# Attention scores from two fp32r parts on alternating 64-row halves of TensorE, with the maxima's product in front of the scores in each step

## The chip, the core and the metric

The kernel runs on one NeuronCore of a Trainium2 chip. The core has TensorE (matrix products, PE), VectorE (DVE), ScalarE (ACT), GpSimd (POOL) and SyncE (SP, which here only starts transfers), an on-chip memory of 128 partitions (SBUF) and eight accumulator banks (PSUM) that TensorE writes. The metric is the device time of one execution in microseconds (us), lower is better; the time before is the median of three runs.

## What is computed

The input is 16 images of 128 channels and 32 x 32 positions, so 1024 tokens per image. A group normalisation with a channel gate comes first, then attention with 8 heads of 16 dimensions, then a mixture of 8 experts of which each token takes two. The part that matters here, shortened from the reference:

```python
qkvt = x @ W_qkv                        # x: (16, 1024, 128), after a layer norm
q, k, v, t = jnp.split(qkvt, 4, axis=-1)
q, k, v, t = map(to_heads, (q, k, v, t))            # 8 heads of 16
dots = jnp.einsum('bhid,bhjd->bhij', q, k) * scale  # 16 ** -0.5
attn1 = jax.nn.softmax(dots, axis=-1)
out1 = jnp.einsum('bhij,bhjd->bhid', attn1, v)
# out2: t smeared with fixed weights exp(-|i-j|/e); out = [out1, out2] @ W_out + b_out
```

## The kernel before, in words

**Stages.** From about 76 to 1966 us the kernel works on attention, one image after the other. The experts follow, as 71 blocks of 512 token rows, and a last pass adds the results. The expert products already use the type fp32r, with 128 x 128 weights and 512 columns (L978 to L980).

**Scores before.** The fp32 values of q and k are split into three bf16 parts each. Six products of parts make up one score, and they are stacked along the contraction: 6 x 16 = 96 rows (`SHIFT_ROW`), plus 3 rows for the row maximum in three parts against ones (`STACK` = 99). So one product on 96 or 99 rows gives an fp32-like score. The split is made by `split` on GpSimd (four passes over 128 x 1024 for q, four for k; VectorE does it for image 0). SP writes the parts to DRAM (`rows_to_dram`) and reads them back as stacks (`load_stacks`), since they change partitions on the way.

**Each score is computed twice.** `full_scores` (L825) computes one unit, one head and 128 queries against all 1024 keys, as two products of 512 columns into one of two bank pairs; `maximum` (VectorE, L1359) reduces the unit to its row maxima. 64 units make an image. After 32 units `turn_maxima` turns the maxima (L832), `shift` (VectorE) splits them, and `load_shift` (SP) writes them into the query stack as extra rows. `scores` (L845) then computes the transposed scores less the maximum, two products of 512 columns per step into two banks, `weights` (ScalarE, L1114) takes the exponential of each, and `values` (L857) multiplies every two steps the four probability tiles with the values: four fp32 products on 32-column tiles of the array, next to each other (eight records in the trace, as fp32 products with 128 x 512 operands show up as two parts).

**Order.** All engines follow an order written out by hand. An image has 64 steps. In step s of image `it` TensorE issues `scores(it, s + 1)` (two products), the unit of maxima that lies 40 steps ahead (two products), in odd steps `values`, and then side work by tables: transposes of 4 x 128 columns in steps 0, 2 (`turn_x`), 4 (`turn_o`), 6, 8 (`back_o`), 12, 14 (`back_n`), 42, 44 (`turn_t2`), 48, 50, 52 (`turn_o`); the dispatch product in 62; 512-column fp32 products in 16, 18 (q), 20, 22 (k), 32, 36 (`project_out`), 54 to 60 (`values_and_z`, two of them as four 128-column products); small ones in 25 and 57 (`turn_maxima`) and 53 (logits). A side result goes through the one side bank and is copied out by ScalarE or VectorE two to four steps later. A pair of steps, in this text, reaches from the end of one `values` group to the end of the next; the side work of an even step stands in its middle.

**Waits around the change.** A score product waits until the exponential has read its bank (`exp_done`). A unit of maxima waits until the unit two before it is reduced (`max_done`). The first score product of each half image waits for the shift rows (`shift_in`). `projected` (ScalarE, L1079) copies q and k out of the side bank for `split`.

Of the kernel before, what the change touches and what calls it, by code (L numbers as in the profile page):

```python
# [7 lines left out]
F32 = mybir.dt.float32  # L8
BF16 = mybir.dt.bfloat16
# [6 lines left out]
P = 128  # L16
# [21 lines left out]
PAIRS = 6  # L38
SHIFT_ROW = PAIRS * DH
STACK = SHIFT_ROW + 3  # L40
# [61 lines left out]
DCT_Y = (0, 1, 0, -1, 3, 0, 2, 0)  # L102

# [81 lines left out]
def build(nc, a, out):  # L185
# [3 lines left out]
    with ExitStack() as ctx:  # L189
# [46 lines left out]
        max_parts = sb("max_parts", [GROUP_ROWS, 3, P], BF16)  # L236
        max_rest = sb("max_rest", [GROUP_ROWS, P])
# [15 lines left out]
        q_parts = sb("q_parts", [P, 3, TOK], BF16)  # L253
        k_parts = sb("k_parts", [P, 3, TOK], BF16)
# [5 lines left out]
        def stack(n):  # L260
            return big[0:STACK, n * BIG_Q:(n + 1) * BIG_Q].bitcast(BF16).rearrange("p (h t) -> p h t", h=HEADS)

# [74 lines left out]

        q_rows = dram("q_rows", (PAIRS, P, TOK), BF16)
        k_rows = dram("k_rows", (PAIRS, P, TOK), BF16)
# [10 lines left out]
        memset_done = sem("memset_done")  # L350
        root_done = sem("root_done")
# [20 lines left out]
        qk_split = sem("qk_split")  # L372
        rows_out = sem("rows_out")
# [62 lines left out]
        LATE_INC = 16 * len(late_consts)  # L436
        CONST_INC = 16 * len(consts)
        ROWS_INC = PAIRS * 16
        STACK_INC = 2 * 16
        SHIFT_INC = 3 * 16  # L440
# [15 lines left out]
        def _(sp):  # L456
# [10 lines left out]
            def rows_to_dram(k):  # L467
                sp.wait_ge(qk_split, 2 * k + 1)
                if k:
                    for g in range(GROUPS):  # L470
                        sp.wait_ge(stack_in[(k - 1) % 2][g], ((k - 1) // 2 + 1) * STACK_INC)
                sp.dma_start(q_rows[0:3].rearrange("s p t -> p s t"),
                             q_parts[:, 0:1, :].broadcast_to([P, 3, TOK])).then_inc(rows_out, 16)
                sp.dma_start(q_rows[3:5].rearrange("s p t -> p s t"),
                             q_parts[:, 1:2, :].broadcast_to([P, 2, TOK])).then_inc(rows_out, 16)
                sp.dma_start(q_rows[5], q_parts[:, 2, :]).then_inc(rows_out, 16)
                sp.wait_ge(qk_split, 2 * k + 2)
                sp.dma_start(k_rows[0:3].rearrange("s p t -> p s t"), k_parts[:, 0:3, :]).then_inc(rows_out, 16)
                sp.dma_start(k_rows[3:5].rearrange("s p t -> p s t"), k_parts[:, 0:2, :]).then_inc(rows_out, 16)
                sp.dma_start(k_rows[5], k_parts[:, 0, :]).then_inc(rows_out, 16)  # L480

            def load_stacks(k, g):
                sp.wait_ge(rows_out, (k + 1) * ROWS_INC)
                if k >= 2:
                    sp.wait_ge(score_ready, 2 * (k - 2) * STEPS + (g + 1) * STEPS)
                heads = slice(g * GROUP, (g + 1) * GROUP)
                for stk, rows in ((q_stack, q_rows), (k_stack, k_rows)):
                    by_row = rows.rearrange("s (d h) t -> (s d) h t", h=HEADS)
                    sp.dma_start(stk[k % 2][0:SHIFT_ROW, heads, :],
                                 by_row[:, heads, :]).then_inc(stack_in[k % 2][g], 16)  # L490

            def load_shift(k, g):
                sp.wait_ge(max_split, 2 * k + g + 1)
                for j in range(3):
                    sp.dma_start(q_stack[k % 2][SHIFT_ROW + j:SHIFT_ROW + j + 1, g * GROUP:(g + 1) * GROUP, :]
                                 .rearrange("p h (t q) -> p (h t) q", q=P),
                                 max_parts[:, j, :]).then_inc(shift_in, 16)
# [86 lines left out]
        def _(pool):  # L584
# [7 lines left out]
            def clear(n):  # L592
                link(pool.memset(v_aug[n], 0.0))
                link(pool.memset(v_aug[n][:, :, :, DH:DH + 1], 1.0))
                link(pool.memset(k_stack[n][SHIFT_ROW:STACK, :, :], 1.0))
# [7 lines left out]

            link(pool.memset(minus_half[:, :], -0.5))
# [1055 lines left out]
```

## Time and profile before

| | |
|---|---|
| median of 3 runs | 2513.67 us (2505.27 to 2515.43) |
| profiled execution | 2517.94 us, span 2516.0 us |
| TensorE busy | 2175.5 us (86%) |
| VectorE busy | 1883.6 us (75%) |
| ScalarE busy | 1453.4 us (58%) |
| GpSimd busy | 1116.9 us (44%) |
| mean granted TensorE clock | 0.944 |

The profile is taken on one execution. Busy time of TensorE counts a product from its start to a modelled end, and successive products overlap in it, so the distance between starts tells more than the duration. What a group of instructions waited for is shown as idle time in front of it with the instruction that ended it.

### The profile page before, as it was taken

How to read it: one execution, taken by the hardware profiler on the slowest of the kernel's cores; microseconds unless marked ns; L12 is line 12 of the kernel's file. 1: busy time of each engine (PE TensorE's matmuls, PEld its weight loads, DVE VectorE, ACT ScalarE, POOL GpSimd, SP SyncE). 2: the span in 40 equal slices, each digit the busy share in tenths (PEclk: the TensorE clock that was granted, in tenths of full speed). 3: DMA queues.
4: the chain of work that ended last, by engine and by line, in shares of the span. 5: the costliest groups of instructions: out<-in, count | busy, mean ns of one | idle time of the engine just before them, and what ended most of it. 6: DMA issues, size and time to landing. Idle time of an engine off the chain costs nothing.

```text
span 2516.0 us, 33117 instructions
## 1 busy us (share of the span) xinstructions
PE 2175.5 (86%) x11552; PEld 897.6 (36%) x11552; DVE 1883.6 (75%) x2555; ACT 1453.4 (58%) x2833; POOL 1116.9 (44%) x1240
## 2 busy tenths in 40 slices
PE   2589999999999999999999999999999447778843
PEld 1223333323333333323233333333232136666633
DVE  7877888888888888888888888888882256666732
ACT  1157767767776767767776767666667213444420
POOL 4303316163544526162535435263142446777764
PEclk9889999999999999999999999999998668998975
DMA  5412222231313132231313132322012058666659
GB/s 182 133 43 77 66 79 91 80 110 30 107 35 102 44 102 74 79 106 31 110 33 104 36 101 68 93 74 64 17 52 76 26 170 286 208 195 201 213 172 341
DMA packets 109926, 264.83 MB, mean 105 GB/s; under 512 B 23048, under 2 KB 40912, under 8 KB 103184
## 3 DMA queue, kind: packets, MB, share of 16 engines
q1 hardware_dynamic: 87600, 217.77, 27.6%
q0 software_dynamic: 17280, 35.95, 4.1%
q10 hardware_dynamic: 4880, 8.99, 0.9%
q8 instruction: 92, 1.51, 0.3%
q14 instruction: 74, 0.61, 0.1%
HBM read 154.63 MB, written 111.56 MB: 106 GB/s over the span
## 4 chain that ended last, share of the span: by engine, by line
PE 57%; POOL 12%; ACT 10%; DMA 8%; DVE 5%; issue 5%; SPq 1%; ACTq 0%; POOLq 0%; DVEq 0%
PE ps L857 17%; PE ps L845 15%; PE ps L825 12%; ACT region L1114 8%; POOL y_dram L732 5%; PE ps L802 2%; DMA big<-w_dram 2%; DMA y_dram<-region 2%; DVE row_max L1359 2%; DMA region<-y_dram 2%; POOL norm_v L625 1%; POOL region L629 1%; POOL region L628 1%; ACT region L1121 1%; PE ps L889 1%
## 5 line engine op out<-in xcount | busy, mean ns | idle before, releaser
L1359 DVE TENSOR_REDUCE row_max<-ps 128x1 f32<-128x1024 f32 x1024 | 1239.7, 1220 | 270.8 <-PE ps L825 239.4
L1114 ACT ACTIVATE region<-ps 128x512 f32<-128x512 f32 x2048 | 1112.7, 596 | 528.9 <-PE ps L845 509.6
L845 PE MATMUL ps<-big 99*128 99x512 bf16 x2048 | 666.1, 387 | 44.4 <-DMA big<-max_parts 12.8
L825 PE MATMUL ps<-big 96*128 96x512 bf16 x2048 | 617.6, 383 | 29.6 <-DMA big<-k_rows 18.7
L857 PE MATMUL ps<-region 128*32 128x512 f32 x4096 | 551.1, 610 | 0.7 <-ACT region L1114 0.7
L845 PEld LDWEIGHTS ps<-big 99*128 99x128 bf16 x2048 | 159.8, 98 | 696.1 <-ACT region L1114 649.9
L732 POOL DMA_INDIRECT y_dram<-region x284 | 272.8, 960 | 126.2 <-issue 81.6
L617 POOL TENSOR_TENSOR norm_v<-norm 128x8 f32<-128x8 f32 x32 | 6.7, 210 | 650.2 <-DVE norm L1350 650.1
L676 POOL DMA_INDIRECT xs_dram<-region,slot x256 | 254.9, 996 | 81.2 <-issue 71.8
L825 PEld LDWEIGHTS ps<-big 96*128 96x128 bf16 x2048 | 199.4, 99 | 245.3 <-DVE row_max L1359 30.2
L978 PE MATMUL ps<-big 128*128 128x512 f32 x284 | 128.3, 452 | 73.1 <-DMA big<-w_dram 72.5
L1186 ACT ACTIVATE region<-ps,big 128x512 f32<-128x512 f32 x71 | 48.9, 689 | 209.2 <-PE ps L980 209.2
L857 PEld LDWEIGHTS ps<-region 128*32 128x32 f32 x4096 | 80.8, 108 | 215.6 <-issue 214.8
L1588 DVE TENSOR_SCALAR big<-ps,big 128x512 fp32r<-128x512 f32 x142 | 105.7, 745 | 34.2 <-PE ps L980 33.9
L1578 DVE TENSOR_TENSOR big<-ps,big 128x512 fp32r<-128x512 f32 x71 | 49.1, 692 | 97.1 <-ACT big L1180 78.0
L979 PE MATMUL ps<-big 128*128 128x512 f32 x284 | 120.9, 426 | 0.0
L980 PE MATMUL ps<-big 128*128 128x512 f32 x284 | 120.6, 425 | 0.0
L1591 DVE SCALAR_TENSOR_TENSOR big<-ps,big 128x512 fp32r<-128x512 f32 x142 | 106.6, 751 | 5.0
L651 POOL TENSOR_TENSOR chosen<-pick 128x64 bf16<-128x64 f32 x16 | 5.1, 319 | 209.9 <-DVEq L1451 209.9
L978 PEld LDWEIGHTS ps<-big 128*128 128x128 f32 x284 | 58.3, 205 | 96.7 <-DMA big<-w_dram 84.6
L1028 PE MATMUL ps<-ident,region 128*128 128x128 f32 x128 | 31.5, 428 | 63.0 <-POOL region L739 63.0
L1194 ACT ACTIVATE region<-ps,region 128x128 f32<-128x128 f32 x284 | 80.7, 373 | 4.1 <-DMA y_dram<-region 3.6
(195 smaller groups left out, 2189.4 us busy)
## 6 DMA issues: line engine op xcount, KB each, us to landing
big<-w_dram SPq DMA_DIRECT2D x71, 514.0 KB, 4.6
big<-q_rows SPq DMA_DIRECT2D x32, 768.0 KB, 5.7
big<-k_rows SPq DMA_DIRECT2D x32, 768.0 KB, 8.0
region<-xs_dram SPq DMA_DIRECT2D x71, 264.0 KB, 2.8
region<-y_dram SPq DMA_DIRECT2D x16, 1024.0 KB, 10.5
region<-in_x SPq DMA_DIRECT2D x28, 512.0 KB, 9.3
q_rows<-q_parts SPq DMA_DIRECT2D x16, 768.0 KB, 3.8
k_rows<-k_parts SPq DMA_DIRECT2D x16, 768.0 KB, 3.5
```

Of the source, the lines that this page charges most:

```text
L676: pool.indirect_dma_start(xs_dram[:, :], bass.IndirectOffsetOnAxis(ap=slot[:, n * TILES + t:n * TILES + t + 1], axis=0), n2_row[:, t, :], ...
L732: pool.indirect_dma_start(y_dram[:, :], bass.IndirectOffsetOnAxis(ap=xs[b % XS_BUFS][:, j, INDEX_COL:INDEX_COL + 1].bitcast(I32), axis=0), ...
L825: mm = pe.matmul(ps[:, M_BANK + 2 * (n % 2) + c, :], q_stack[k % 2][0:SHIFT_ROW, h, t * P:(t + 1) * P], k_stack[k % 2][0:SHIFT_ROW, h, c * ...
L845: pe.matmul(ps[:, E_BANK + i, :], k_stack[k % 2][:, h, t * P:(t + 1) * P], q_stack[k % 2][:, h, c * BANK:(c + 1) * BANK], start=True, stop ...
L857: mm = pe.matmul(ps[32 * r:32 * r + 32, O_BANK, :], v_aug[k % 2][:, t, g * GROUP + r, :], probs[:, u % 2, r, :], start=(t == 0), stop=(t = ...
L978: pe.matmul(dst, w[:, high_at:high_at + P], high, start=start, stop=False)
L979: pe.matmul(dst, w[:, high_at:high_at + P], low, start=False, stop=False)
L980: return pe.matmul(dst, w[:, low_at:low_at + P], high, start=False, stop=stop)
L1114: act.activation(probs[:, u % 2, 2 * p + i, :], ps[:, E_BANK + i, :], ACT.Exp, scale=DH ** -0.5).then_inc(exp_done, 1)
L1359: dve.tensor_reduce(row_max[:, n:n + 1], ps[:, at:at + 2, :], AX.XY, ALU.max).then_inc(max_done, 1)
L1588: dve.tensor_scalar(h_high[b % 2][f], src, w[:, NEG_B1 + f:NEG_B1 + f + 1], None, ALU.max).then_inc(h_high_done, 1)
L1591: dve.scalar_tensor_tensor(h_low[b % 2][f], src, w[:, NEG_B1 + f:NEG_B1 + f + 1], h_high[b % 2][f].bitcast(F32), ALU.max, ALU.subtract).th ...
```

## The change

The parts become fp32r: two parts of q and k (`PARTS`), three products of parts (`PAIRS`), so 48 rows, and 2 rows for the maximum (`STACK` = 50). The stacks are laid out in two halves (`LANES`): heads 0 and 1 of each group of four lie in partitions 0 to 49, heads 2 and 3 in 64 to 113. A product therefore addresses 64 rows by 128 columns of the array. `max_unit` reorders the units of maxima within half an image so that they alternate between the halves. In the loop of TensorE the first unit of maxima is issued by halves in front of the two score products: M, S, M, S.

ScalarE now rounds the first part straight from the side bank (`parts[:, 0]`) and then copies the full value, and takes over the wait for the last image's row transfers. GpSimd and, for image 0, VectorE only subtract. `shift` has two operations instead of four. The rows of ones come from a small tile by four transfers from ScalarE's queue, instead of GpSimd's memsets. The stacks are loaded in four transfers per call instead of two, the shift rows in four instead of three.

```diff
@@
-PAIRS = 6
+PARTS, PAIRS = 2, 3
+LANES = 2
+LANE = P // LANES
+LANE_HEADS = GROUP // LANES
 SHIFT_ROW = PAIRS * DH
-STACK = SHIFT_ROW + 3
+STACK = SHIFT_ROW + PARTS
@@
+def max_unit(n):
+    g, i = divmod(n, GROUP_ROWS)
+    lane = 1 - i % LANES
+    of_lane, t = divmod(i // LANES, TILES)
+    return g * GROUP + lane * LANE_HEADS + of_lane, t
@@ stacks
+        def lane_of(h):
+            return h % GROUP // LANE_HEADS
+        def lane_rows(stk, h, rows):
+            at = lane_of(h) * LANE
+            return stk[at:at + rows, h // GROUP * LANE_HEADS + h % LANE_HEADS, :]
@@ split, on GpSimd
-                if k:
-                    pool.wait_ge(rows_out, k * ROWS_INC)
-                link(pool.tensor_copy(parts[:, 0, :], full))
-                link(pool.tensor_tensor(full, full, parts[:, 0, :], ALU.subtract))
-                link(pool.tensor_copy(parts[:, 1, :], full))
-                pool.tensor_tensor(parts[:, 2, :], full, parts[:, 1, :], ALU.subtract).then_inc(qk_split, 1)
+                pool.tensor_tensor(parts[:, 1, :], full, parts[:, 0, :].bitcast(F32), ALU.subtract).then_inc(qk_split, 1)
@@ full_scores(unit, c): one half of a unit
+                h, t = max_unit(n)
...
+                mm = pe.matmul(ps[:, M_BANK + 2 * (n % 2) + c, :],
+                               lane_rows(q_stack[k % 2], h, SHIFT_ROW)[:, t * P:(t + 1) * P],
+                               lane_rows(k_stack[k % 2], h, SHIFT_ROW)[:, c * BANK:(c + 1) * BANK], start=True, stop=True)
@@ scores(k, s, i): one of the two products
+                h = g * GROUP + LANE_HEADS * p + i
...
+                pe.matmul(ps[:, E_BANK + i, :], lane_rows(k_stack[k % 2], h, STACK)[:, t * P:(t + 1) * P],
+                          lane_rows(q_stack[k % 2], h, STACK)[:, c * BANK:(c + 1) * BANK], start=True,
+                          stop=True).then_inc(score_ready, 1)
@@ the loop of TensorE
-                    if here and s + 1 < STEPS:
-                        scores(it, s + 1)
-                    if nxt and s + 1 == STEPS:
-                        scores(it + 1, 0)
-                    for unit in max_units(it, s):
-                        full_scores(unit // STEPS, unit % STEPS)
+                    units = list(max_units(it, s))
+                    for c in range(HALVES):
+                        if units:
+                            full_scores(units[0], c)
+                        if here and s + 1 < STEPS:
+                            scores(it, s + 1, c)
+                        if nxt and s + 1 == STEPS:
+                            scores(it + 1, 0, c)
+                    for unit in units[1:]:
+                        for c in range(HALVES):
+                            full_scores(unit, c)
@@ projected, on ScalarE
                 if c == 0 and k:
                     act.wait_ge(qk_split, 2 * k)
+                    act.wait_ge(rows_out, k * ROWS_INC)
+                act.activation(parts[:, 0, c * BANK:(c + 1) * BANK], side, ACT.Copy).then_inc(q_high, 1)
+                q_highs[0] += 1
+                act.wait_ge(q_high, q_highs[0])
                 act.activation(dst[:, c * BANK:(c + 1) * BANK], side, ACT.Copy).then_inc(side_free, 1)
@@ shift, on VectorE
                 then(dve.tensor_scalar(max_parts[:, 0, :], turned_max, -1.0, None, ALU.mult))
-                then(dve.scalar_tensor_tensor(max_rest[:, :], turned_max, -1.0, max_parts[:, 0, :], ALU.mult, ALU.subtract))
+                then(dve.scalar_tensor_tensor(max_parts[:, 1, :], turned_max, -1.0, max_parts[:, 0, :].bitcast(F32),
+                                              ALU.mult, ALU.subtract))
+                dve.sem_inc(max_split, 1)
                 dve.sem_inc(side_free, 1)
-                then(dve.tensor_copy(max_parts[:, 1, :], max_rest[:, :]))
-                dve.tensor_tensor(max_parts[:, 2, :], max_rest[:, :], max_parts[:, 1, :],
-                                  ALU.subtract).then_inc(max_split, 1)
```

On TensorE, a pair of steps with the transposes `turn_o` in its middle, between two `values` groups (L857), before: L845 is a score product, L825 one for the maxima, L865 the transposes.

```order
L857 MATMUL ps<-region 32x512 x4
L845 MATMUL ps<-big 128x512 x2
L825 MATMUL ps<-big 128x512 x2
L865 MATMUL ps<-ident,region 128x128 x4
L845 MATMUL ps<-big 128x512 x2
L825 MATMUL ps<-big 128x512 x2
L857 MATMUL ps<-region 32x512 x4
```

The same pair after the change: L846 is a product for the maxima, L867 a score product, L888 the transposes, L880 the values.

```order
L880 MATMUL ps<-region 32x512 x4
L846 MATMUL ps<-big 128x512
L867 MATMUL ps<-big 128x512
L846 MATMUL ps<-big 128x512
L867 MATMUL ps<-big 128x512
L888 MATMUL ps<-ident,region 128x128 x4
L846 MATMUL ps<-big 128x512
L867 MATMUL ps<-big 128x512
L846 MATMUL ps<-big 128x512
L867 MATMUL ps<-big 128x512
L880 MATMUL ps<-region 32x512 x4
```

The number of products is the same; the two kinds alternate, and a score product is now the last one before the transposes and before the values.

On GpSimd, the work for image 1 between its first normalisation and the edges of image 0, before:

```order
L629 TENSOR_TENSOR region<-region,norm_v 128x1024
L640 CAST q_parts<-region 128x1024
L641 TENSOR_TENSOR region<-region,q_parts 128x1024
L642 CAST q_parts<-region 128x1024
L643 TENSOR_TENSOR q_parts<-region,q_parts 128x1024
L640 CAST k_parts<-region 128x1024
L641 TENSOR_TENSOR region<-region,k_parts 128x1024
L642 CAST k_parts<-region 128x1024
L643 TENSOR_TENSOR k_parts<-region,k_parts 128x1024
L656 TENSOR_TENSOR region<-region,edges 128x2x64
```

And after:

```order
L655 TENSOR_TENSOR region<-region,norm_v 128x1024
L656 TENSOR_TENSOR region<-region,norm_v 128x1024
L665 TENSOR_TENSOR q_parts<-region,q_parts 128x1024
L665 TENSOR_TENSOR k_parts<-region,k_parts 128x1024
L678 TENSOR_TENSOR region<-region,edges 128x2x64
```

Of eight passes over q and k two are left; the casts to the first part are ScalarE's now.

## Rows read from the trace of the kernel before

**Rows 1.** From the page: the span, and the granted clock in 40 equal slices.

```profile
span 2516.0 us, 33117 instructions
...
PEclk9889999999999999999999999999998668998975
```

**Rows 2.** Stretches: length, busy us (count) of PE, PEld, DVE, ACT, POOL; clock, DMA, GB/s.

```profile
133.00:1895.30 1762.30, 1717.22 (x9467) 584.81 (x9468) 1473.08 (x1893) 1227.97 (x2290) 696.15 (x815) 1.00 0.23 71
...
888.73:1003.23 114.50, 111.93 (x625) 38.69 (x622) 96.33 (x126) 80.44 (x150) 49.24 (x59) 1.00 0.24 75
```

**Rows 3.** Timeline of a plain pair: start, duration, engine, line, operation, count, idle before.

```profile
1012.57 1.06 PE L857 MATMUL ps<-region 128*32 128x512 f32 x8
1013.56 0.61 PE L845 MATMUL ps<-big 99*128 99x512 bf16 x2
...
1013.99 2.23 ACT L1114 ACTIVATE region<-ps 128x512 f32<-128x512 f32 x4 [1.09 <-PE ps L845]
...
1014.64 0.88 PE L845 MATMUL ps<-big 99*128 99x512 bf16 x2
...
1015.36 0.60 PE L825 MATMUL ps<-big 96*128 96x512 bf16 x2
1015.88 1.06 PE L857 MATMUL ps<-region 128*32 128x512 f32 x8
```

**Rows 4.** Timeline of TensorE in a pair with L876 and one with transposes L883.

```profile
1006.55 0.60 PE L845 MATMUL ps<-big 99*128 99x512 bf16 x2
...
1007.43 1.02 PE L876 MATMUL ps<-region,wo 128*128 128x512 f32 x2
...
1008.29 0.59 PE L845 MATMUL ps<-big 99*128 99x512 bf16 x2
...
1010.24 0.60 PE L845 MATMUL ps<-big 99*128 99x512 bf16 x2
...
1016.88 0.61 PE L845 MATMUL ps<-big 99*128 99x512 bf16 x2
...
1017.76 0.60 PE L883 MATMUL ps<-ident,region 128*128 128x128 f32 x4
...
1018.20 0.64 PE L845 MATMUL ps<-big 99*128 99x512 bf16 x2
...
1020.20 0.61 PE L845 MATMUL ps<-big 99*128 99x512 bf16 x2
```

**Rows 5.** The expert stage: its clock as in rows 2, and TensorE's timeline after a wait.

```profile
2140.00:2160.00 20.00, 14.72 (x77) 11.81 (x75) 14.09 (x21) 8.45 (x24) 15.15 (x16) 1.00 0.63 192
...
2157.22 0.49 PE L978 MATMUL ps<-big 128*128 128x512 f32 x1 [1.06 <-DMA big<-w_dram]
2157.56 0.39 PE L979 MATMUL ps<-big 128*128 128x512 f32 x1
2157.79 0.40 PE L980 MATMUL ps<-big 128*128 128x512 f32 x1
```

**Rows 6.** Groups by line, weight loads: count, busy us, mean ns of one, idle before.

```profile
L845 PEld LDWEIGHTS ps<-big 99*128 99x128 bf16 x2048 | 159.8, 98 | 696.1 <-ACT region L1114 649.9 <-issue 41.9
...
L978 PEld LDWEIGHTS ps<-big 128*128 128x128 f32 x284 | 58.3, 205 | 96.7 <-DMA big<-w_dram 84.6 <-DVE big L1591 0.8 <-ACT region L1186 0.6
```

**Rows 7.** Timeline: the transposes behind GpSimd's normalisation.

```profile
965.02 0.66 PE L797 MATMUL ps<-ident,region 128*128 128x128 f32 x4 [0.74 <-POOL region L629]
```

**Rows 8.** Groups by line: ScalarE's copies of q and k.

```profile
L1079 ACT ACTIVATE region<-ps 128x512 f32<-128x512 f32 x64 | 38.7, 604 | 15.5 <-PE ps L802 15.5
```

**Rows 9.** Timeline of the start: GpSimd's last split, stack load and shift rows, first scores.

```profile
115.32 2.12 POOL L643 TENSOR_TENSOR k_parts<-region,k_parts 128x1024 bf16<-128x1024 f32 x1
...
122.99 0.33 SPq L489 DMA_DIRECT2D big<-q_rows  x1
...
123.83 2.02 SPq L495 DMA_DIRECT2D big<-max_parts  x3
...
132.98 1.01 PE L845 MATMUL ps<-big 99*128 99x512 bf16 x2 [12.84 <-DMA big<-max_parts]
```

More of the change, by code:

```diff
@@ L435, in build @@
         FROM_SP = 8
-        LATE_INC = 16 * len(late_consts)
+        ones_rows = [k_stack[n][lane * LANE + SHIFT_ROW:lane * LANE + STACK, :, :] for n in range(2) for lane in range(LANES)]
+        LATE_INC = 16 * (len(late_consts) + len(ones_rows))
         CONST_INC = 16 * len(consts)
-        ROWS_INC = PAIRS * 16
-        STACK_INC = 2 * 16
-        SHIFT_INC = 3 * 16
+        ROWS_INC = 2 * PARTS * 16
+        STACK_INC = 2 * LANES * 16
+        SHIFT_INC = PARTS * LANES * 16
         SENT_INC = TILES * 16
@@ L485, in load_stacks @@
                     sp.wait_ge(score_ready, 2 * (k - 2) * STEPS + (g + 1) * STEPS)
[L486 to L490, printed above, removed]
+                for lane in range(LANES):
+                    first_head = g * GROUP + lane * LANE_HEADS
+                    for stk, rows in ((q_stack, q_rows), (k_stack, k_rows)):
+                        by_row = rows.rearrange("s (d h) t -> (s d) h t", h=HEADS)
+                        sp.dma_start(stk[k % 2][lane * LANE:lane * LANE + SHIFT_ROW,
+                                                g * LANE_HEADS:(g + 1) * LANE_HEADS, :].bitcast(F32),
+                                     by_row[:, first_head:first_head + LANE_HEADS, :]).then_inc(stack_in[k % 2][g], 16)
             def load_shift(k, g):
                 sp.wait_ge(max_split, 2 * k + g + 1)
[L494 to L497, printed above, removed]
+                for lane in range(LANES):
+                    for j in range(PARTS):
+                        row = lane * LANE + SHIFT_ROW + j
+                        sp.dma_start(q_stack[k % 2][row:row + 1, g * LANE_HEADS:(g + 1) * LANE_HEADS, :]
+                                     .rearrange("p h (t q) -> p (h t) q", q=P).bitcast(F32),
+                                     max_parts[lane * LANE_HEADS * TILES:(lane + 1) * LANE_HEADS * TILES, j, :]
+                                     .bitcast(F32)).then_inc(shift_in, 16)
             rows_to_dram(0)
@@ L1041, in _ @@
                 act.dma_start(tile, src).then_inc(late_in, 16)
+            act.wait_ge(ones_done, 1)
+            for rows in ones_rows:
+                act.dma_start(rows.rearrange("p h (n c) -> p (h n) c", c=P).bitcast(F32),
+                              ones_r[:, :].bitcast(F32).unsqueeze(1).broadcast_to([PARTS, HEADS // LANES * TILES, P])
+                              ).then_inc(late_in, 16)
             def excite():
@@ L1488, in _ @@
                 dve.wait_ge(side_free, side_at[kind, 0, 1] + 1)
[L1489 to L1492 removed]
+                dve.tensor_tensor(parts[:, 1, :], full, parts[:, 0, :].bitcast(F32), ALU.subtract).then_inc(qk_split, 1)
             for n in range(9, len(X_LATER)):
```

79 lines of the change are left out of this document (35 added, 44 removed).

## Prediction

> **What bounds the kernel now.** I first read the span and the granted clock [rows 1], then the stretch in which attention runs [rows 2]. From 133 to 1895 us the clock is 1.00, which is the 2.4 GHz level, and TensorE is busy for 1717 of 1762 us, VectorE for 1473, ScalarE for 1228. One image takes 114.50 us. So TensorE's order of work sets the pace, but "busy" also covers waiting between products, so I cut the order of one image into its 32 pairs of steps (from one group of value products to the next) and timed them. In the notation below S is a score product, M a product for the maxima, V the value group.
>
> A plain pair (nothing but S S M M S S M M V) takes 3.32 us [rows 3]. Its products do not fill it; a chain does: first S at 1013.56, exponentials from 1013.99 (0.43 later), whose two results let the second pair of S start at 1014.64 and 1015.14 (the 0.88 us of that row less one product's 0.38), 1.15 after 1013.99; then that S (0.22), M M until V at 1015.88 (0.52), and V's slot of 1.00. Sum 3.32.
>
> A pair that holds four transposes also takes 3.32, and one with a 512-column fp32 product 3.69 [rows 4]. These are full: S S M M takes 0.88, so 0.22 each; the transposes 0.44; the fp32 product 0.86; V's slot 0.99; and entering V costs 0.08 more than two products (0.52 against 0.44). 8 x 0.22 + 0.86 + 0.99 + 0.08 = 3.69, exactly as read. With transposes it is 3.27, which hides just under the chain's 3.32. By the tables of steps an image has 13 pairs with transposes or the dispatch product, 10 with large fp32 products, and 9 plain ones; the trace of the image from 888.73 to 1003.23 shows the same count.
>
> **What the change does to a plain pair.** All rows of a product now lie in 64 rows of the array. In the steady order both kinds of product of a step lie on the same half (step s multiplies S of step s+1 on half (s+1)%2, and M of unit n, with n and s of equal parity, on half 1 - n%2). So within a step there is nothing to run side by side; only the last S of a step and the first M of the next could overlap, and in a plain pair that place isn't on the chain. I take nothing for the overlap.
>
> A product of this type costs 0.23 us from start to start in the expert stage, at a granted clock of 1.00 there as well, and 0.34 when its weights could not be loaded ahead [rows 5]; its weight load takes 205 ns against 98 for bf16 [rows 6]. So a waiting product costs 0.11 more, which the bf16 ones don't show. The new chain is: M in front of the first S, behind V, 0.34; S to exponential 0.43; 1.15 as before; the last S, which waits, 0.34; into V 0.08; V 0.99. Sum 3.33. The M pair that leaves the end of the chain (0.44) comes back as one M in front and two exposed loads. Without any exposed load the sum would be 3.11, with one more 3.44. I take 3.32, no change, since the expert row is the only one of this type.
>
> **A pair with side work** is full, so each addition counts. 8 x 0.23 + 0.11 (first M behind V) + 0.99 + 0.08 + 0.44 = 3.46 with transposes, 3.88 with the large product. To this comes a change of tile shape: S and M work on 64x128 tiles, side work on the full 128x128, and the side work stands between two S/M blocks (the excerpts of the order, above). No row shows this switch. The bounds are 0 and the price of the nearest one, V's: its two rounds should take 0.86 like the two parts of the large product, so its slot of 0.99 and the 0.08 make 0.21 for the round trip, plus 0.11 for the slower load on the way back, 0.32. I take 0.32, because V's switch is the only switch in this trace. That gives 3.78 (+0.46 over 3.32) and 4.20 (+0.51 over 3.69).
>
> The Trainium skill, TensorEngine Tiling (Array Packing), section Tiling Modes, says that changing the tiling mode, not just the tile, drains the engine. It gives no price; by that rule the switch is not free, and V's 0.21 agrees that some switches are not.
>
> **Sum.** Per image 13 x 0.46 + 10 x 0.51 + 9 x 0 = 11.1 us. A longer pair swallows waits that are there now: the product behind GpSimd's normalisation waited 0.74 us [rows 7]; with smaller ones I take off 1.0, leaving 10.1. Steps with maxima run from 133 to 1895 us, 15.4 images of 114.5: +155 us. With free switches it would be 13 x 0.14 + 10 x 0.19 - 1.0 = 2.7 per image, +42 us. The last 20 pairs have no M: two exposed loads each, +4 us.
>
> **Other edits.** ScalarE gets a second copy per q and k half, 64 of 0.60 us [rows 8]. They stand where it otherwise idles: 1.09 us per pair [rows 3], and in the pairs that now become longer; 0, and up to +10 us if the cover is gone. The wait for the row transfers moves from GpSimd to ScalarE; the exponentials are queued behind it, but it concerns the transfers of the image before, a whole image (114 us) earlier: 0. GpSimd loses three of four passes per split, VectorE two of four small operations per shift: neither is what TensorE waits for in steady state, 0. The stacks carry the same bytes in twice as many transfers, the shift rows come in four transfers instead of three, 0 where they have an image's slack. At the start it matters: TensorE waited 12.84 us for the first shift rows, which SP could issue only at 123.83, behind a stack load that waited for GpSimd's split [rows 9]. That split is now short: between 0 and -9 (issue to 132.98); I take -5. The longer copy chain before the first maxima (+0.6 x 4) and the shorter VectorE split cancel. The products in front also ask for their PSUM bank earlier, and now an S stands behind them. VectorE is busy for 96.33 of 114.50 us [rows 2], and the pairs get longer, so I take 0, with +40 as the upper bound (0.3 in each plain pair).
>
> Forecast: 2517.94 (profiled execution; span 2516.0) + 155 + 4 - 5 = 2672. The median of the runs is 4.3 below the profiled execution, so 2668.
>
> **Rivals.**
> (a) Switches are cheap. V's extra time may belong to its 32-column tiles alone. +42, +2, -5: 2553. Against it: V is the only evidence, and it shows a price; for it: weights for the other half may be loaded while the array streams.
> (b) Not slower: the halves are free. A half's weights load under any other work, so neither the switch nor a load is exposed. Then plain pairs follow the shortened chain, 3.11 (-0.21), transposes 3.35 (+0.03), large 3.77 (+0.08): -0.7 per image, -11, and -5 at the start: 2498. It decides from the point where the chain's gain (9 x 0.21) exceeds the fuller pairs. Against it: the first expert product after a wait shows 0.34 [rows 5].
> (c) Loads on one half don't hide. Then six of eight products cost 0.42 instead of 0.23: +1.14 in the full pairs, +0.84 in plain ones (3.02 of products + 1.14 against 3.32), 34 us per image more: about 3190. The expert rows speak against it: 205 ns loads into the same rows hide under a spacing of 0.23 [rows 5, 6].
> The rule for (c) stands in the Trainium skill, TensorE: Matmul & The Clock Gate, section Part 3: a weight load overlaps a running product only if their row groups differ. The expert rows contradict it for full-height products; on halves no row here tests it.
> (d) The halves do overlap more than I see, if M and S of a step lay on different halves. By the formulas of the code they don't; only in the first 40 steps of image 0 some do. Included in (b).
>
> **How the numbers follow.** Forecast with its neighbourhood (2600 to 2730) 0.58; (a) 0.20; (b) 0.10; (c) 0.05; something else 0.07, such as a lower granted clock because of half the rows. The range takes in (a) and the upper bounds for ScalarE and VectorE: 2535 to 2735. A measurement of this kernel can tell 0.5%, some 12 us, from no change. Faster: (b) mostly, 0.08; same 0.06; slower 0.86.
>
> **What would show it.** In the changed profile: plain pairs near 3.3 us, pairs with transposes near 3.8, large ones near 4.2; the products' spacing within a step 0.23; a gap before and behind each side group. Pairs with transposes at 3.4 would show (a), plain pairs at 3.1 (b), spacing of 0.42 within a step (c). A wait of maxima products on VectorE would be the upper bound above. If the first score product starts at 133 us again, the -5 is wrong. I would be wrong altogether if M and S of a step overlapped, seen as starts a few ns apart.

## The result, and the profile after

The changed kernel takes **3777.03 us** (median of four runs, 3748.51 to 3850.24) against 2512.71 us for the kernel before: ratio 1.5016, 95% interval 1.4931 to 1.5102. The profiled execution, 3850.24 us with a span of 3848.4 us, is the slowest of the four, 2.7% above the fastest, and the ratio leaves it out. The forecast was 2668 and the range 2535 to 2735, so the time lies far outside.

The page of the profile after, to be read against [rows 1]: the span, busy time and share of each engine, the granted clock in 40 slices, and the group of the value products (count, busy us, mean ns of one, idle before).

```profile
span 3848.4 us, 33090 instructions
...
PE 3553.4 (92%) x11552; PEld 1692.5 (44%) x11552; DVE 1872.1 (49%) x2485; ACT 1579.2 (41%) x2897; POOL 968.8 (25%) x1149
...
PEclk9855555585555557575757575555555755589995
...
L880 PE MATMUL ps<-region 128*32 128x512 f32 x4096 | 901.1, 969 | 0.3 <-ACT region L1153 0.3
```

The line of the clock is what the forecast did not have. Before, it stood at 9 from 189 to 1887 us; now it is 5 in most slices of attention, which is the 1.2 GHz level. The other lines agree: VectorE's busy time is what it was (1872.1 against 1883.6 us), but its share fell from 75% to 49%, and the value products, which the change does not touch, have a mean of 969 ns (610 before).

Two stretches of TensorE's timeline show a pair of steps with transposes at either level (columns: start, duration, engine, line, operation, count; L846 is M, L867 is S, L880 is V). First at 2.4 GHz:

```profile
1518.36 0.50 PE L846 MATMUL ps<-big 48*128 48x512 f32 x1
1518.70 0.39 PE L867 MATMUL ps<-big 50*128 50x512 f32 x1
1518.94 0.39 PE L846 MATMUL ps<-big 48*128 48x512 f32 x1
...
1519.49 0.66 PE L906 MATMUL ps<-ident,region 128*128 128x128 f32 x4
1520.07 0.49 PE L846 MATMUL ps<-big 48*128 48x512 f32 x1
...
1521.21 1.06 PE L880 MATMUL ps<-region 128*32 128x512 f32 x8
1522.21 0.50 PE L846 MATMUL ps<-big 48*128 48x512 f32 x1
```

and at 1.2 GHz:

```profile
1412.18 0.79 PE L846 MATMUL ps<-big 48*128 48x512 f32 x1
...
1413.20 0.62 PE L846 MATMUL ps<-big 48*128 48x512 f32 x1
1413.63 0.62 PE L867 MATMUL ps<-big 50*128 50x512 f32 x1
1414.19 1.11 PE L888 MATMUL ps<-ident,region 128*128 128x128 f32 x4
...
1417.23 1.93 PE L880 MATMUL ps<-region 128*32 128x512 f32 x8
1419.10 0.79 PE L846 MATMUL ps<-big 48*128 48x512 f32 x1
```

The pair takes 3.85 us in one and 6.92 in the other (from the M that begins the excerpt to the M that ends it). Successive products start 0.23 and 0.43 apart, and V, which is the same in every kernel here, has a duration of 1.06 and 1.93. So V's duration tells the level without the record of the clock. I cut the attention of every kernel by it, from one V to the next (512 of them); "high" and "low" below are the sums of these distances. Before: 1799 us high, 29 low. After: **409 high, 2751 low**.

Where the clock changes, after (two stretches as in [rows 2], the clock is the third number from the end; then the timeline of the fall at 1541 us):

```profile
1300.00:1490.00 190.00, 190.00 (x539) 85.42 (x539) 81.97 (x108) 77.11 (x133) 38.01 (x51) 0.50 0.09 20
1500.00:1540.00 40.00, 39.10 (x196) 18.20 (x199) 30.20 (x38) 26.26 (x48) 6.79 (x11) 1.00 0.36 82
```

```profile
1539.93 1.07 PE L880 MATMUL ps<-region 128*32 128x512 f32 x8
1540.92 1.95 PE L912 MATMUL ps<-gate_c,region 128*128 128x8 f32 x16
...
1545.19 0.79 PE L846 MATMUL ps<-big 48*128 48x512 f32 x1
```

TensorE is busy for all but 7 of the 2751 low us; the clock is not low for want of work in the queue. From 1492 us on it rises in the plain pairs after `turn_maxima` (1492, then 1673, 1854, 2035, 2216, 3042) and falls each time, 55 us later, right after the logits (L912), 16 records that stream 8 columns each. Two earlier spells at the high level end elsewhere: one of 5 us at the start (162 to 167), and one from 770 to 842 us, which ends after an M that waited 1.77 us for VectorE (836.30). Outside of attention little changed: the first V starts at 143.42 (138.93 before), and from the last V to the end it is 544.9 us (548.8).

### The profile page after: what moved, and what is told of

Its sections match the earlier page's. It is cut to its first block, busy times and chain, and to the rows that moved or that the text cites. A ratio compares the mean times of both kernels' runs of the same rounds, so it can differ in the third digit from the quotient of the medians.

```text
span 3848.4 us, 33090 instructions
## 1 busy us (share of the span) xinstructions
PE 3553.4 (92%) x11552; PEld 1692.5 (44%) x11552; DVE 1872.1 (49%) x2485; ACT 1579.2 (41%) x2897; POOL 968.8 (25%) x1149
## 4 chain that ended last, share of the span: by engine, by line
PE 84%; POOL 5%; DMA 4%; issue 3%; ACT 1%; DVE 1%; SPq 1%; ACTq 0%; POOLq 0%; DVEq 0%
PE ps L846 25%; PE ps L880 22%; PE ps L867 21%; POOL y_dram L754 4%; PE ps L824 3%; PE ps L836 2%; PE ps L832 2%; PE ps L888 1%; DMA big<-w_dram 1%; DMA y_dram<-region 1%; PE ps L899 1%; PE ps L912 1%; ACT region L1153 1%; DMA region<-y_dram 1%; PE ps L819 1%
## 5 line engine op out<-in xcount | busy, mean ns | idle before, releaser
L1153 ACT ACTIVATE region<-ps 128x512 f32<-128x512 f32 x2048 | 1194.2, 596 | 1705.5 <-PE ps L867 1694.6
L846 PE MATMUL ps<-big 48*128 48x512 f32 x2048 | 1215.9, 655 | 28.6 <-DMA big<-k_rows 19.9
L867 PE MATMUL ps<-big 50*128 50x512 f32 x2048 | 1187.1, 592 | 18.8 <-ACT region L1153 13.5
L846 PEld LDWEIGHTS ps<-big 48*128 48x128 f32 x2048 | 537.9, 282 | 1009.2 <-DVE row_max L1399 605.3
L880 PE MATMUL ps<-region 128*32 128x512 f32 x4096 | 901.1, 969 | 0.3 <-ACT region L1153 0.3
L867 PEld LDWEIGHTS ps<-big 50*128 50x128 f32 x2048 | 599.3, 295 | 263.2 <-ACT region L1153 140.0
L880 PEld LDWEIGHTS ps<-region 128*32 128x32 f32 x4096 | 98.0, 133 | 273.4 <-issue 273.0
L684 POOL TENSOR_TENSOR region<-region 128x1024 f32<-128x1024 f32 x16 | 37.9, 2370 | 344.5 <-DVE region L1445 344.5
L665 POOL TENSOR_TENSOR q_parts<-region,q_parts 128x1024 fp32r<-128x1024 f32 x15 | 35.5, 2368 | 352.7 <-ACT region L1118 352.7
```

Source lines behind the costliest of these rows:

```text
L846: mm = pe.matmul(ps[:, M_BANK + 2 * (n % 2) + c, :], lane_rows(q_stack[k % 2], h, SHIFT_ROW)[:, t * P:(t + 1) * P], lane_rows(k_stack[k % ...
L867: pe.matmul(ps[:, E_BANK + i, :], lane_rows(k_stack[k % 2], h, STACK)[:, t * P:(t + 1) * P], lane_rows(q_stack[k % 2], h, STACK)[:, c * BA ...
L880: mm = pe.matmul(ps[32 * r:32 * r + 32, O_BANK, :], v_aug[k % 2][:, t, g * GROUP + r, :], probs[:, u % 2, r, :], start=(t == 0), stop=(t = ...
L1153: act.activation(probs[:, u % 2, 2 * p + i, :], ps[:, E_BANK + i, :], ACT.Exp, scale=DH ** -0.5).then_inc(exp_done, 1)
```

## The experiments

Theory R says that the array rows that the score products use decide whether the clock stays up, 96 and 99 of 128 before and 48 and 50 now. Its rivals are the type fp32r (or its weight loads), the tiles of 64 rows with their switches, and the new order. Where no number of runs is given, an experiment was run once.

**1. All rows, everything else as changed.** Products read partitions 0 to 111 or 113, so both halves at once.

```diff
-            at = lane_of(h) * LANE
-            return stk[at:at + rows, ...]
+            return stk[0:LANE + rows, ...]
```

> The changed kernel (order, type, split, transfers as they are), but each score product and each product for the maxima reads rows 0 to 111 or 113 of the stacks, both halves, so it works on the full 128x128 array. What it computes is therefore the sum of two heads' scores, and the rows of ones are zero, so no maximum is subtracted; the output is not the reference's. The large stack tile is cleared once at the start on GpSimd (up to 30 us more). Theory R (the granted clock falls because the products use only 64 rows of the array): clock 1.00 through attention, plain pair 3.3 us, pair with transposes about 3.5, large about 3.9 (no change of tile shape): 2540 to 2620 us. Rival T (the type fp32r with its long weight loads lets the clock fall) and rival O (the alternating order does it): clock stays near 0.55, about 3700 us.

Measured 2564.93 us. Its page:

```profile
span 2563.1 us, 33091 instructions
...
PEclk9899999999999999999999999999999759999975
```

1873 us high, 8 low. One edit to the rows takes 1285 us off the profiled execution and 1212 off the median, with the type and the order as in the changed kernel. Type and order fall as rivals. The tile of 64 rows does not yet: it went away together with the short products. The experiment also separates the price of the tile switches, since here all products but V use 128 x 128 tiles. A pair with transposes takes 3.51 (1290.60 to 1294.10) against 3.85, one with a large product 3.93 or 3.94 against 4.32, a plain one 3.34 against 3.33:

```profile
1290.60 0.50 PE L846 MATMUL ps<-big 112*128 112x512 f32 x1
...
1291.64 0.60 PE L888 MATMUL ps<-ident,region 128*128 128x128 f32 x4
1292.00 0.48 PE L846 MATMUL ps<-big 112*128 112x512 f32 x1
...
1294.10 0.50 PE L846 MATMUL ps<-big 112*128 112x512 f32 x1
```

The transposes' slot is 0.36 here (1291.64 to 1292.00) and 0.58 above (1519.49 to 1520.07). The switch to another tile shape and back costs 0.34 to 0.38 us.

**2 to 4. Fewer rows with bf16.** The kernel before, with 64, 66, or 48 and 50 of its rows in the score products.

```diff
-q_stack[k % 2][0:SHIFT_ROW, h, ...], k_stack[k % 2][0:SHIFT_ROW, h, ...]
+q_stack[k % 2][0:64, h, ...], k_stack[k % 2][0:64, h, ...]
```

> The kernel before, with its order, its bf16 and its load on the queues, but each score product and each product for the maxima reads only rows 0 to 63 of the stacks (two of six partial products and the maximum are left out of the score; the output is not the reference's). Same columns, same counts. Theory R: the granted clock falls to 0.5 for most of attention and the time rises to 3300 to 3800 us. Rivals T and O: clock 1.00; the time stays within 1.5% of before, plus at most 0.2 us per pair for the change of tile shape (up to 2600 us).

> As the 64-row variant of the kernel before, but 66 rows: two more rows, and the product then addresses the whole 128x128 array instead of a 64x128 tile. If it is the tile shape (which halves of the array are switched on) that the clock follows, this run is like before: 1.00 and about 2515 us. If it is the number of rows that carry data, it is like the 64-row variant: clock near 0.5, over 3200 us.

> The kernel before with products on rows 0 to 47 (maxima) and 0 to 49 (scores) of its bf16 stacks: as many rows as in the changed kernel, where the earlier variant had 64. Part of the score and the maximum are left out; the output is not the reference's. The 64-row variant lost its clock only in short stretches behind the logits (2851 us). If each row counts, 48 rows lose it for long stretches: 3300 to 3800 us. If it is the type fp32r that keeps the changed kernel down, this run is like the 64-row one: 2800 to 2900 us.

| rows in a product | type | tile | us | high | low |
|---|---|---|---|---|---|
| 96 / 99 (before) | bf16 | 128 x 128 | 2513 | 1799 | 29 |
| 112 / 114 (first experiment) | fp32r | 128 x 128 | 2565 | 1873 | 8 |
| 66 | bf16 | 128 x 128 | 2636 | 1670 | 276 |
| 64 | bf16 | 64 x 128 | 2851 | 1507 | 656 |
| 48 / 50 | bf16 | 64 x 128 | 3582 | 581 | 2304 |
| 48 / 50 (after) | fp32r | 64 x 128 | 3777 | 409 | 2751 |

The fewer rows, the more of attention runs low, and with 48 and 50 rows bf16 does nearly as badly as fp32r. The run with 48 and 50 rows came out as expected. Those with 64 and 66 met neither side of their expectations: 64 rows should have cost 3300 us or at most 2600, 66 rows 2515 or over 3200. Between 66 and 64 rows the tile changes as well, so the step from 276 to 656 may belong to either. From 64 to 48 and 50 rows the tile is the same, and the low time goes from 656 to 2304; there the rows alone do it. The 2851 us hold a price of the switch too: at the full clock the pairs with transposes take 3.51 to 3.52 and the large ones 3.98 to 3.99, against 3.32 and 3.69 [rows 4]. With 66 rows they take 3.32 and 3.69, as before, so that product does use the full tile. In the kernel with 64 rows, too, the clock falls at the logits (1139.39), which before stay without effect in every image but the last, where no M is left:

```profile
1139.39 1.95 PE L889 MATMUL ps<-gate_c,region 128*128 128x8 f32 x16
...
1142.33 2.07 PE L810 MATMUL ps<-wvz,region 128*128 128x128 f32 x8
```

**5. The changed kernel in the old order, S S M M.**

> The changed kernel with only its order undone: S S M M again, still on 64-row halves in fp32r. The output is the reference's. Theory R: the order has no part in the clock, so it stays near 0.5 for most of attention, 3500 to 3900 us. Rival O: the clock recovers, 2700 us.

Measured 4111.09 us, above the expected 3500 to 3900, 58 high and 3362 low. The order isn't what lowers the clock. What the order is worth can't be read here, since the two kernels were at the high level for different stretches.

**6. The old kernel in the new order.** Six bf16 products of parts, full height, but M S M S.

```diff
-                    if here and s + 1 < STEPS:
-                        scores(it, s + 1)
-                    for unit in max_units(it, s):
-                        full_scores(unit // STEPS, unit % STEPS)
+                    for c in range(HALVES):
+                        if units:
+                            full_scores(units[0], c)
+                        if here and s + 1 < STEPS:
+                            scores(it, s + 1, c)
```

> The kernel before (bf16, full height) with one part of the change: in each step the product for the maxima stands in front, M S M S. The output is the reference's. By the chain: M 0.22, score to exponential 0.43, 1.15, last score 0.22, into V 0.08, V 0.99 give 3.09 for a plain pair instead of 3.32; pairs with transposes are full at 3.27 (from 3.32), large ones stay at 3.69. Per image 9 x 0.23 + 13 x 0.05 = 2.7 us, 42 us in all: about 2470 us, 0.983 of before, clock 1.00. Rival O (the alternating order itself lets the clock fall or makes VectorE's reductions late): 2510 us or more.

Measured 2473.21 us (2470.73 to 2481.43, four runs) against 2510.54: ratio 0.9857, interval 0.9835 to 0.9879. This one edit out of the change **beats both kernels**, by 1.4% the one before. A plain pair of it takes 3.10 instead of 3.32, one with transposes 3.28 and a large one 3.71, where 3.09, 3.27 and 3.69 were expected:

```profile
1106.96 0.39 PE L825 MATMUL ps<-big 96*128 96x512 bf16 x1
...
1108.74 0.39 PE L846 MATMUL ps<-big 99*128 99x512 bf16 x1
1109.06 1.06 PE L858 MATMUL ps<-region 128*32 128x512 f32 x8
1110.06 0.39 PE L825 MATMUL ps<-big 96*128 96x512 bf16 x1
```

After the last S (here L846) V follows in 0.32 us; before, S was followed by M M and V came 0.52 after these began [rows 3]. The chain of the prediction, S to exponentials to S to V, is the one that binds, and its shortening by the M pair is real. This kernel also has the only wait above 1.4 us in the attention of a kernel with 96 and 99 rows, and the clock falls behind it, for 4.8 us:

```profile
302.30 0.39 PE L825 MATMUL ps<-big 96*128 96x512 bf16 x1 [2.02 <-DVE row_max L1365]
...
305.89 1.94 PE L858 MATMUL ps<-region 128*32 128x512 f32 x8
...
310.66 1.07 PE L858 MATMUL ps<-region 128*32 128x512 f32 x8
```

**7. Everything on one half.** The changed kernel with all products on partitions 0 to 49.

```diff
-            at = lane_of(h) * LANE
+            at = 0
```

> The changed kernel with all products on rows 0 to 49: heads 2 and 3 of each group are computed from the data of heads 0 and 1, so the output is not the reference's. Everything else, the transfers too, is as in the changed kernel. If the alternation between halves matters to the clock (each half is idle half of the time either way), it differs from 3770 us by more than 5%; Theory R says it does not: 3650 to 3900 us.

Measured 4180.16 us: none high, 3488 low. This lies above the expected 3650 to 3900, and by the expectation's own measure (5% from 3770 us) the alternation does matter: not as the cost of the clock, since without it things are worse, but as something that gives part of it back. Why is not shown. This run also shows that the record of the clock can be wrong. A stretch of it, and TensorE's timeline within:

```profile
1450.00:1550.00 100.00, 100.00 (x277) 43.40 (x273) 43.70 (x58) 41.26 (x73) 23.63 (x34) 1.00 0.12 23
```

```profile
1499.83 1.93 PE L880 MATMUL ps<-region 128*32 128x512 f32 x8
...
1502.29 0.62 PE L867 MATMUL ps<-big 50*128 50x512 f32 x1
1502.72 0.62 PE L846 MATMUL ps<-big 48*128 48x512 f32 x1
```

The stretch says 1.00, yet V takes 1.93 and the products are 0.43 apart, as in the low stretch of the changed kernel, where the record says 0.50. The experiments with 48 and 50 rows in bf16 and in the old order have such stretches too (their pages show 9 to about 1400 and 1700 us, where every V before 1389 and 1768 us takes 1.93). All sums of high and low here go by V's duration for that reason. The Trainium skill, TensorE: Matmul & The Clock Gate, section Part 1, warns that the events of the clock in a trace have been seen to be unreliable; this run agrees, with 1.00 beside 1.93.

**8. M and S on opposite halves.** In the changed kernel both products of a step lie on the same half. One line puts them on opposite ones.

```diff
-    lane = 1 - i % LANES
+    lane = i % LANES
```

> The changed kernel with one formula turned: the product for the maxima lies on the other half than the score product of its step, so M and S can run side by side. The output is the reference's. If halves run side by side, the M and S of a step start a few ns apart instead of 0.23 us, and four products take about 0.46 us instead of 0.92. Theory R with the clock following the rows in use at a time: the clock recovers in part or wholly; at 1.00 throughout, pairs are bound by the chain, 3.1 to 3.3, and the time is 2450 to 2600. If the clock stays at 0.5: values group 1.9, products 0.86 per step: about 3000 us. If halves don't run side by side at all: unchanged, 3770 us.

Measured 2536.05 us, 1620 high and 226 low. The two start together:

```profile
1301.66 0.49 PE L846 MATMUL ps<-big 48*128 48x512 f32 x1
1301.66 0.49 PE L867 MATMUL ps<-big 50*128 50x512 f32 x1
...
1302.32 0.66 PE L894 MATMUL ps<-ident,region 128*128 128x128 f32 x4
```

Four products and the way into the side work take 0.66 us instead of 1.13 (1518.36 to 1519.49 above), plain pairs and pairs with transposes 3.10, pairs with a large product 3.38 where nothing else waits, and with 98 rows at work at once the clock mostly stays up. The low stretches are in the first image (to 228 us), in the last one, and 14 short ones of 4 to 15 us between them. Only one of these (1728) follows the logits. The other 13 follow a new wait of 1.8 to 1.9 us, that of the transposes (L819) for GpSimd's normalisation:

```profile
1313.62 0.66 PE L819 MATMUL ps<-ident,region 128*128 128x128 f32 x4 [1.90 <-POOL region L656]
...
1314.87 1.68 PE L880 MATMUL ps<-region 128*32 128x512 f32 x8
```

So this wait costs its own length and a spell at the low clock. Each q and k product waits another 0.47 us.

**9. The same with the transposes behind the normalisation and the q and k products issued later** (`AT_PREP` from (0, 2), (12, 14), (16, 18), (20, 22) to (0, 2), (16, 18), (20, 23), (26, 29)), to see what these waits are worth.

> The changed kernel with the product for the maxima and the score product of a step on opposite halves, and the four pieces of the last normalisation passes spread out (0-2, 16-18, 20-23, 26-29 instead of 0-2, 12-14, 16-18, 20-22), so that the transposes of the next image need not wait 1.90 us for GpSimd. The same computation as before. Theory (rows in use at a time hold the clock, halves overlap): plain and transpose pairs stay at 3.10, large ones near 3.4; the 1.90 wait goes and perhaps part of the four 0.47 waits for ScalarE's copies of q and k; 2 to 4 us per image less than the 2536 of the version without the new timing, and the short spells at the lower clock remain: 2475 to 2510. If halves in use at once do not hold the clock, it would lie above 2600. If GpSimd is the limit whatever its timing, it stays at 2536.

Measured 2514.28 us against 2509.55, ratio 1.0024 (1.0009 to 1.0038), slightly above the expected 2475 to 2510. The wait for GpSimd is gone from the steady images, and with it all 13 falls behind it. Waits for the exponential remain around the q and k products (up to 0.72 us). From logits to logits an image takes 109.1 us where the clock stays up (1256.95 to 1366.07) and 112.5 where it falls, against 114.5 before. From the first logits to the thirteenth that is 1319.8 us against 1374.1, a gain of 54 us. It is lost again at both ends: the first logits come 31 us later than before, and from the thirteenth to the last V it takes 25 us more. Of the 180 us at the low clock most lie there, in the first image (157 to 222) and in the last one (from 1876).

**10 and 11. Are the logits the trigger?** Their eight products write 64 columns each (the eight of the gate, eight times over) instead of 8; the readers take the first eight. Once on experiment 9, once on the changed kernel.

```diff
-mm = pe.matmul(ps[:, SIDE_BANK, t * EXPERTS:(t + 1) * EXPERTS], t2[...], gate_c[:, :], ...)
+mm = pe.matmul(ps[:, SIDE_BANK, t * 64:(t + 1) * 64], t2[...], gate_c[:, :], ...)    # gate_c 64 wide
```

> The retimed version with opposite halves, and the eight products of the logits write 64 columns each (the gate's eight columns eight times over) instead of 8; the readers take the first eight. The same result. Theory T (the clock falls in the logits because few columns stream in these 2 us): the pair with the logits goes from 8.07 to about 5.3 in the images where it fell, the spells at 0.50 in the steady images go, 2 to 4 us per affected image: 2480 to 2505. Rival (the logits only happen to stand where the sum of earlier work falls short, or the fall comes from the weights, not the columns): the falls stay, 2510 to 2520. The start of image 0 at the lower clock stays in both.

> The changed kernel with nothing altered but the 64 columns per product of the logits. Theory T: the clock holds after the logits where it was high before them, so once it is up it stays up; attention mostly at full clock, 2750 to 3200. Rival (the score products of 64 rows alone are too little and the logits only set the moment of the fall): it falls elsewhere, 3600 to 3850 as before.

On experiment 9: 2505.14 us against 2509.80, ratio 0.9982 (0.9968 to 0.9995), so below experiment 9 with intervals that don't meet, and at the upper end of the expected 2480 to 2505. The four falls that experiment 9 has at logits (381, 1366, 1479 and 1806 us) are gone, while the logits take hardly longer, 2.00 against 1.97. Both have short low stretches left in the first images (at 247 and 341 us here), and the long ones at the start and in the last image. First experiment 9, then this one:

```profile
1366.07 1.97 PE L912 MATMUL ps<-gate_c,region 128*128 128x8 f32 x16
...
1372.27 1.93 PE L880 MATMUL ps<-region 128*32 128x512 f32 x8
```

```profile
1373.30 2.00 PE L912 MATMUL ps<-gate_c,region 128*128 128x64 f32 x16
...
1377.64 1.06 PE L880 MATMUL ps<-region 128*32 128x512 f32 x8
```

On the changed kernel: 3634.75 us in its one run, 710 high and 2236 low. The time is the one that the rival gave; of theory T only the part on the logits holds. No fall stands at the logits any more (at 2235.83 it passes them at 2.4 GHz). But apart from a spell of 5 us at the start, the clock falls in three other places while M and S are both issued, near 525, 1310 and 2317 us, each time right after an M that waited 1.66 to 1.75 us for VectorE:

```profile
2316.88 0.50 PE L846 MATMUL ps<-big 48*128 48x512 f32 x1 [1.74 <-DVE row_max L1400]
...
2318.03 1.94 PE L880 MATMUL ps<-region 128*32 128x512 f32 x8
```

So what stood before a fall in the steady images of the half-height kernels was either the logits or a wait of 1.66 to 1.92 us, for VectorE here and at 836.30 in the changed kernel, for GpSimd in experiment 8. The logits don't lower the clock of the kernel before or of the first experiment as long as M are issued. Such waits those two don't have at all (none above 1.4 us), and the one of 2.02 us in experiment 6, at full height, was followed by a fall too. What differs is how long the low level lasts: 4.8 us there, and here 651, 876 and 435 us (529 to 1180, 1311 to 2187, 2318 to 2753). The logits or a wait give the moment of the fall; that the logits are enough for it, and that the clock then stays low, comes with the few rows.

## Why the prediction was wrong, step by step

**The step that failed** is the clock. "From 133 to 1895 us the clock is 1.00" was read from the trace of before and carried over in silence; every term of the sum is a duration at 2.4 GHz. A lower clock "because of half the rows" stood in the remainder of 0.07, with no time of its own and outside the range. It should have been a rival with a price, and the rows had one: the products would use 48 to 50 rows where 96 and 99 held the clock [rows 2], and no stretch of the trace showed the clock with half-height products. What the runs showed in its place: 2751 of the 3160 us of attention at the 1.2 GHz level, and 8 of 1881 when the same products, in the same type and order, read 112 and 114 rows (experiment 1). By an estimate, twice the 3.78 and 4.20 of the sum, the full pairs would come near 7.5 to 8.4 at half the clock; they took 6.91 and 7.87.

**How much it is.** One image all at the low level takes 220.58 us (from the logits at 602.91 to those at 823.49 in experiment 11). At 2.4 GHz an image of the changed kernel would take the 118.15 of the first experiment (1182.99 to 1301.14) plus 13 x 0.34 and 10 x 0.38 for the switches, 126.4. So the 2751 low us would be 2751 x 126.4 / 220.58 = 1576, and the clock costs 1175 of the 1332 us that were added to the span. What is left is 157 us; worked out the other way, 15.4 x (126.4 - 114.5) = 183. The forecast had 154. These are estimates from the rows named, as no run of the changed kernel kept the clock. The span is that of the profiled execution; the median lies 73 us below it, and its share of low time is not recorded.

**The terms at the full clock:**

| | predicted | measured after |
|---|---|---|
| plain pair | 3.32 | 3.33 |
| with transposes | 3.78 | 3.85 |
| with a large product | 4.20 | 4.32 |
| spacing on one half | 0.23 | 0.23 |
| M behind V | 0.34 | 0.34 |
| switch to side work and back | 0.32 | 0.34 to 0.38 |

- The sum of the plain pair held, in part by luck. Its parts read 0.33 for M, 1.08 to the third S, 0.57 to the fourth, 0.34 into V and 1.00 for V. From the first S to the fourth that is 1.65 where the forecast had 1.58 (0.43 and 1.15), and from the fourth S into V 0.34 where it had 0.42 (0.34 and 0.08), so two errors cancel:

```profile
1504.07 0.66 PE L846 MATMUL ps<-big 48*128 48x512 f32 x2
1504.40 0.39 PE L867 MATMUL ps<-big 50*128 50x512 f32 x1
1504.64 0.39 PE L846 MATMUL ps<-big 48*128 48x512 f32 x1
...
1505.48 0.49 PE L867 MATMUL ps<-big 50*128 50x512 f32 x1 [0.22 <-ACT region L1153]
1505.82 0.40 PE L846 MATMUL ps<-big 48*128 48x512 f32 x1
1506.05 0.41 PE L867 MATMUL ps<-big 50*128 50x512 f32 x1
1506.39 1.07 PE L880 MATMUL ps<-region 128*32 128x512 f32 x8
```

- That a switch has a price was right, and so was V's slot as its measure; 0.32 was 0.02 to 0.06 short. This refutes rival (a) for the mechanism, and with it (b). The Trainium skill, TensorEngine Tiling (Array Packing), section Tiling Modes, says that a change of the tiling mode drains the engine. The trace agrees in that the change costs time, 0.34 to 0.38 us there and back; that a drain is what takes it, no record shows.
- Rival (c) is refuted: on one half products start 0.23 apart with weight loads of 0.19 us. The Trainium skill, TensorE: Matmul & The Clock Gate, section Part 3, has the rule that a load overlaps a running product only if the row groups differ. It does not hold for these products, and the measurement decides. The same section also says that a load into a background weight buffer is pulled ahead of running products; these numbers would fit that, but no run tests it.
- Rival (d) was right on where M and S lie. It put the idea aside as not in the code, which was true; one line makes it so, and it is worth 0.2 us per plain pair, 0.75 per pair with transposes and over 0.9 per large one (experiment 8).
- The start: TensorE's wait for the first shift rows fell from 12.84 to 5.23 us, inside the 0 to 9 of the forecast, and SP issued them as soon as they were split (134.34). But the first S starts at 138.29, against 132.98 before and 128 by the forecast: the products ahead of it ran low, and `turn_maxima` came at 132.42 instead of 119.73. The -5 was wrong in its result.
- GpSimd's and ScalarE's edits cost nothing that the trace shows; at the low clock both have slack.

**What stays open:** why the low level lasts for hundreds of microseconds although TensorE is busy throughout, whether the tile's shape adds to the rows' effect between 66 and 64, why one fixed half is worse than two in turn, and why the clock rises in those plain pairs. The low time of every kernel comes from one execution, so only large differences count.

## What to carry to other kernels

The clock is a term of the sum. A change that has the matrix array use fewer rows per product, at the same number of products, needs a line on what the clock does, with the price of the low level beside it (here the whole pair times 1.6 to 1.8). Where half-height products are wanted, put two that are issued together on opposite halves. And when a change bundles several edits, time them one by one: here the reordering alone gives 0.9857. In the same order, at full height, fp32r takes 2564.93 us (experiment 1) against 2473.21 in bf16 (experiment 6), so the type with its split and transfers costs about 92 us, and the halves cost the rest.

## What the runs showed of the hardware that was not expected

- Attention at the low level, with TensorE busy for all but 1 to 8 us of it: 29 us with 96 and 99 rows, 276 with 66, 656 with 64, 2304 to 2751 with 48 and 50, and 3488 with 48 and 50 rows always on the same half.
- 48 and 50 rows on each half at the same time come close to 96 and 99 in one product: 226 us low against 29, where the same products one after the other have 2751.
- A wait of TensorE of 1.8 to 1.9 us was followed by a spell of 4 to 15 us at the low level in 13 of 13 cases in experiment 8; with the wait gone these spells are gone (experiment 9). One wait of 1.62 us at the start of experiment 9 (241.7) was not followed by any. In the half-height kernel whose M and S share a half, waits of 1.66 to 1.77 us were followed by 435 to 876 us (experiment 11), or 650 (the changed kernel from 842 on).
- The recorded clock read 1.00 in stretches whose products ran at the 1.2 GHz level (experiment 7).
- The excerpt of the plain pair at 1504.07 begins with two M in one record, of 0.66 us, and the next step shows only one M. I read this as the first M of the next step, which lies on the other half, running beside the first M of this one, ahead of the products between them in the program. It is in the plain pairs only; with side work between the steps (1507.39 and 1518.36) M, S, M, S come one by one. Nothing was run to test this reading.
